# Stage 3 of a four-layer cross-attention kernel: rows normalised by quarters inside the last pair of heads, and MLP up and down projections interleaved

## What is computed

```python
def _cross_attention(q_in, kv_in, wq, bq, wk, bk, wv, bv, wo, bo, bias_k, bias_v):   # H=16 heads of K=128
    qh, kh, vh = (q_in @ wq + bq), (kv_in @ wk + bk), (kv_in @ wv + bv)               # split in heads
    kh, vh = concatenate([kh, bias_k]), concatenate([vh, bias_v])                     # one learned key and value
    weights = softmax(einsum('bqhk,bthk->bhqt', qh, kh) / sqrt(K))
    return einsum('bhqt,bthk->bqhk', weights, vh) @ wo + bo
x = x + _cross_attention(layer_norm(x, ln1), ctx, ...)       # sublayer 0
x = x + _cross_attention(layer_norm(x, ln2), ctx, ...)       # sublayer 1
h = layer_norm(x, ln_mlp)
x = x + gelu(h @ w_fc1 + b_fc1) @ w_fc2 + b_fc2              # 256 -> 1024 -> 256
```

## Time and profile before

| | us |
|---|---|
| median of 3 runs | 2165.06 (2163.31 to 2167.14) |
| the profiled execution | 2165.55 |
| its span, first to last instruction | 2163.9 |
| TensorE matmuls busy | 1952.3 (90%) |
| DVE busy | 1288.8 (60%) |
| ACT busy | 1189.3 (55%) |
| POOL busy | 678.0 (31%) |
| granted TensorE clock, mean | 0.966 of full |

### The profile page before, as it was taken

How to read it: one execution, slowest core, us unless ns; L and a number is a source line. 1 busy time by engine, 2 the same in 40 slices (tenths; PEclk the granted TensorE clock), 3 DMA queues, 4 the chain that set the end, 5 groups by cost and what they waited for, 6 DMA issues and landing times.

```text
span 2163.9 us, 43763 instructions
## 1 busy us (share of the span) xinstructions
PE 1952.3 (90%) x14880; PEld 1694.8 (78%) x14880; DVE 1288.8 (60%) x4117; ACT 1189.3 (55%) x3880; POOL 678.0 (31%) x618
## 2 busy tenths in 40 slices
PE   4678899999999988759999999997999999999788
PEld 3457677777777777548999999996899999999687
DVE  3578787878878764434555555556455555555654
ACT  2377787878778776535444444444444444444522
POOL 1233444444434343313222222132212122223444
PEclk8799999999999999869999999999999999999899
DMA  6000000000000000010000000000000000000100
GB/s 254 8 9 6 7 11 4 9 4 4 7 2 4 2 1 1 1 53 16 20 24 15 24 24 19 15 25 16 20 15 24 15 24 24 19 15 15 40 15 24
DMA packets 23663, 45.23 MB, mean 21 GB/s; under 512 B 2400, under 2 KB 10080, under 8 KB 22624
## 3 DMA queue, kind: packets, MB, share of 16 engines
q1 hardware_dynamic: 21440, 32.62, 5.0%
q10 hardware_dynamic: 1440, 8.72, 1.0%
q0 software_dynamic: 640, 2.10, 0.3%
HBM read 41.33 MB, written 2.10 MB: 20 GB/s over the span
## 4 chain that ended last, share of the span: by engine, by line
PE 44%; issue 5%; POOL 3%; DVE 2%; ACT 1%; DMA 0%; POOLq 0%; SPq 0%; DVEq 0%; ACTq 0%
PE general L1613 30%; PE o_psum L1662 5%; PE scores L1650 4%; PE pT_psum L1710 2%; PE general L1769 2%; POOL hT L1250 1%; DVE oT L1595 1%; POOL X L1275 1%; DVE oT L1464 1%; ACT oT L1374 0%; POOL w_qk L1235 0%; DMA raw_vrows<-vrows_dram 0%; POOL w_v L1235 0%; POOL probs L1259 0%; PE general L1624 0%
## 5 line engine op out<-in xcount | busy, mean ns | idle before, releaser
L489 POOL TENSOR_TENSOR probs<-probs,rsums 128x512 f32<-128x512 f32 (+1 forms) x288 | 282.7, 994 | 503.7 <-DVE rsums L691 502.9
L1259 POOL TENSOR_TENSOR probs<-probs,rsums 128x512 f32<-128x512 f32 x128 | 133.2, 1040 | 766.4 <-DVE rsums L1457 766.4
L525 ACT ACTIVATE probs<-negated,negmax 128x128 f32<-128x128 f32 (+1 forms) x768 | 325.4, 431 | 12.4 <-DVE negmax L682 12.1
L1366 ACT COPY probsT<-pT_psum 128x512 f32<-128x512 f32 x128 | 74.9, 585 | 291.1 <-PE pT_psum L1710 291.1
L964 PE MATMUL pT_psum<-ident,probs 128*128 128x128 f32 x1088 | 179.2, 287 | 58.4 <-ACT probsT L533 29.5
L964 PEld LDWEIGHTS pT_psum<-ident,probs 128*128 128x128 f32 x1088 | 127.2, 145 | 114.9 <-issue 68.4
L1613 PE MATMUL general<-hT,w_qk 128*128 128x512 f32 x768 | 207.3, 405 | 3.6 <-POOL hT L1250 3.6
L1613 PE MATMUL general<-w_o,oT 128*128 128x256 f32 x1536 | 195.0, 281 | 16.9 <-DVE oT L1464 16.9
L1613 PEld LDWEIGHTS general<-w_o,oT 128*128 128x128 f32 x1536 | 186.4, 188 | 25.1 <-DVE oT L1464 18.0
L1613 PE MATMUL general<-ctxT,w_qk 128*128 128x512 f32 x768 | 200.6, 397 | 0.0
L1358 ACT ACTIVATE probs<-scores,negmax 128x128 f32<-128x128 f32 x512 | 180.1, 369 | 29.9 <-DVE negmax L1449 29.7
(11 more groups left out here) (173 smaller groups left out, 3910.2 us busy)
## 6 DMA issues: line engine op xcount, KB each, us to landing
raw_qk<-w_qk_dram SPq DMA_DIRECT2D x34, 256.0 KB, 2.7
raw_v<-w_v_dram SPq DMA_DIRECT2D x17, 256.0 KB, 2.7
raw_vrows<-vrows_dram SPq DMA_DIRECT2D x17, 256.0 KB, 3.2
weights_a<-weights_a_dram ACTq DMA_DIRECT2D x2, 2048.0 KB, 18.1
raw_o<-w_o_dram SPq DMA_DIRECT2D x16, 256.0 KB, 2.6
weights_a<-weights_a_dram ACTq DMA_DIRECT2D x3, 1024.0 KB, 9.9
X<-x_dram SPq DMA_DIRECT2D x8, 256.0 KB, 7.8
ctx_in<-ctx_dram SPq DMA_DIRECT2D x8, 256.0 KB, 2.9
```

The costliest lines, as they stand in the source:

```text
L489: nc.gpsimd.tensor_tensor(pr, pr, rsums[:, n % 4, 0:segs].unsqueeze(2).broadcast_to([P, segs, width(kind) // segs]), ALU.mult).then_inc(s[ ...
L525: last = nc.scalar.activation(probs[:, n % PROBS, i * wide:(i + 1) * wide], src[:, i * wide:(i + 1) * wide], ACT.Exp, scale=1.0 if kind == ...
L1259: nc.gpsimd.tensor_tensor(pr, pr, rsums[:, t % 2, :].unsqueeze(2).broadcast_to([P, NB, P]), ALU.mult).then_inc(s["probs_ready"], 1)
```

## The change

1. The loop over sublayers is written out: `open` (first normalisation, as before), 7 pairs, the last pair of sublayer 0 (`turn`), 7 pairs, the last pair of sublayer 1 (`end`). In `turn` and `end` the normalisation of what follows goes by quarters. DVE makes the factors of quarter 0 in step 6 and of quarter 1 in step 7, ahead of that step's additions, those of quarters 2 and 3 around the last additions (`norm_rows`). TensorE transposes quarter 0 in step 7. Normalised rows and their transposed copy have buffers of their own (`xhat_turn`, `raw_hT_turn`), one quarter deep, since `qT` and `kT` are still in use.
2. `turn` keeps the usual table for steps 0 to 3, has keys `k` 3 and 4 in step 4 and `k` 5 behind two output groups in step 5; `q` 4 to 7, `k` 6 and 7 follow the pair, mixed with the last outputs, transposes and first scores.
3. In `end` the loads and splits of weights that nothing uses are left out. The up weights are split in steps 6 and 7 in halves, on ACT and POOL. The down weights are loaded into `kT` and split in halves on ACT and POOL; POOL's part stands after its five low parts of quarter 0.
4. The MLP's up groups of quarter 0 are mixed with the last outputs and the transposes. Then each up group of quarter g+1 is followed by the 12 down matmuls of quarter g for the same 128 hidden columns, into four banks that attention used (`down_sums`). Stores are issued by SP.

```diff
-    if last:
-        return [[*values[0], ("q", 0)], [*values[1], ("k", 0)], [*values[2], ("q", 1)], [*values[3], ("k", 1)],
-                [("q", 2), ("k", 2), ("q", 3)], [("k", 3), *outputs[0][:1]], [outputs[0][1], outputs[1][0]], [outputs[1][1], outputs[2][0]]]
+    if kind == "end":
+        return [[*values[0], ("q", 0)], [*values[1], ("k", 0)], [*values[2], ("k", 1)], [*values[3], ("q", 1)],
+                [("k", 2), ("k", 3), ("q", 2)], [("q", 3), *outputs[0]], outputs[1], [("ln", 0), outputs[2][0]]]
+    if kind == "turn":
+        return [[("q", 0), ("k", 0), *values[0]], [("q", 1), ("k", 1), *values[1]], [("q", 2), ("k", 2), *values[2]], [("q", 3), *values[3]],
+                [("k", 3), ("k", 4)], [*outputs[0], ("k", 5)], outputs[1], [("ln", 0), outputs[2][0]]]
...
+        xhat_turn = sb("xhat_turn3", [P, NB, D])
+        raw_hT_turn = sb("raw_hT_turn3", [P, KC, R])
...
+        down_sums = [scores[0], scores[1], pT_psum, o_psum]
...
# POOL
+                for g in range(G):
+                    for f in range(FC - LATE):
+                        up_low(g, f)
+                    if g == 0:
+                        for half in range(2):
+                            down_weights_low(half)
+                    add_biases(2, g)
...
# DVE
+                def norm_rows(a, g):
+                    norm_factors(slice(NB * g, NB * g + NB), None)
+                    if g > 0:
+                        wait_norm(dve, a, g - 1)
+                    dve.sem_inc(s["wait_passed"], 1)
+                    xhat_rows(a, g)
...
+                        if kind != "pair" and t >= G + 2:
+                            norm_rows(a + 1, t - G - 2)
+                        for key in pair_work(kind)[t]:
...
                     add_out(section, a, loop, G - 2, 1)
                     o_low(a, i, n, STEPS - 1)
-                    if not last:
+                    if kind == "pair":
                         front(n + 1, 0)
+                    else:
+                        norm_rows(a + 1, G - 2)
                     for j in range(2):
                         add_out(section, a, loop, G - 1, j)
+                    if kind != "pair":
+                        norm_rows(a + 1, G - 1)
...
# ACT, in the steps of pair
+                            elif key[0] == "ln":
+                                norm_copies(section, a + 1, 0, [1])
                         copy_pT(n)
+                        if kind != "pair" and t >= G + 2:
+                            xhat_rows(a + 1, t - G - 2)
...
# TensorE
+                pair(0, PAIRS - 1, "turn")
+                transposed("turn", 1, 1)
+                next_queries(4)
+                last_outputs("turn", 0, 0, ATT_UNITS - 1)
+                next_queries(5)
+                transposed("turn", 1, 2)
+                next_queries(6)
+                first_score("turn", 0, 0, ATT_UNITS - 1, [4])
+                keys("turn", 0, 0, 6, 0)
+                transposed("turn", 1, 3)
+                keys("turn", 0, 0, 7, 0)
+                next_queries(7)
...
+                pe.wait_ge(s["w_down_ready"], 2)
+                for g in range(G - 1):
+
+                    for f in range(FC):
+                        up(g + 1, (f,))
+                        wait_upT(g, f)
+                        for b in range(NB):
+                            last = down(g, f, b)
+                        last.then_inc(s["down_read"], 1)
```

More of the change, by code:

```diff
@@ L1299, in _ @@
-                pool.wait_ge(s["stored"], 2 * 16 * G)
+                            add_biases(a, t)
+                        if kind == "end" and t >= G + 2:
+                            up_weights_low(t - G - 2)
+                    if kind != "pair":
+                        for g in range(G):
+                            split_h(a + 1, g)
+                for g in range(G):
+                    split_h(0, g)
+                with pool.Fori(0, PAIRS - 1) as i:
+                    pair(0, i, "pair")
@@ L1348, in copy_q @@
+                    copy_q("open", 0, 0, G - 1, 0, 0)
                 def copy_q(section, a, i, t, head, pair):
@@ L1409, in _ @@
[L1409 to L1418 removed]
+                norm_open()
@@ new lines, in _ @@
+                copy_q("turn", 0, 0, 7, 0, PAIRS)
+                with act.Fori(0, PAIRS - 1) as i:
+                    pair(1, i, "pair")
+                pair(1, PAIRS - 1, "end")
+                norm_copies("end", 2, 1, [0, 1])
+                gelus(0, (0, 1))
+                xhat_rows(2, 2)
+                gelus(0, (2, 3))
+                norm_copies("end", 2, 2, [0, 1])
+                xhat_rows(2, 3)
+                gelus(0, (4, 5))
+                norm_copies("end", 2, 3, [1])
@@ L1420, in _ @@
+                gelus(0, (6, 7))
+                for half in range(2):
+                    down_weights_high(half)
+                for g in range(1, G):
+                    gelus(g, range(FC))
             @block.vector
@@ new lines, in next_queries, with up @@
+                def next_queries(t):
+                    pe.wait_ge(s["hT_ready"], t + 2)
+                    queries("turn", 0, 0, t, 0)
+                def up(g, fs):
+                    for f in fs:
+                        out, filled = wait_free(pe, "end", 1, 0, ("up", g, f))
+                        if f == 0:
+                            pe.wait_ge(s["hT_ready"], 2 * G + g + 2)
+                        split_matmul(out[:, :], lambda part, c: w_up[:, part, c, f * P:(f + 1) * P],
+                                     lambda part, c: hT[:, part, c, quarter(g)]).then_inc(filled, 1)
@@ L1774, in chunked @@
+                for b in range(NB):
+                    for f in range(FC):
+                        if b == 0:
+                            wait_upT(G - 1, f)
+                        last = down(G - 1, f, b)
+                    last.then_inc(s["down_read"], 1)
 def chunked(w):
```

502 lines of the change are left out of this document (283 added, 219 removed).

## The result

The changed kernel takes 2173.93 us, median of 8 runs (2170.33 to 2180.93), the one before 2164.6 us (2160.39 to 2167.14); the ratio is 1.0050, 95% interval 1.0037 to 1.0063. It is slower by 9.3 us. The forecast was 2175 us and slower, so the number came out. Not all of its reasons did: of the two profiled executions, 13.7 us apart (spans 2163.9 and 2177.6 us), stage 3, where the change is, is only 5.6 us longer in the later one.

What follows compares the result with a forecast made beforehand. The prediction saw stage 3's seams bound by a serial normalisation chain leaving TensorE some 46 us idle. Turn +7.5 and end with MLP +2.7 gave +10.2 us on 2165.06, forecast 2175 us, own range 2161 to 2182 (stated 2157 to 2184).

Steps and rivals of the forecast that it cites:

- Step 1: Turn, from the last pair's start to F6: new order of output and key groups costs +5.9 us, at least +5.0.
- F6: Reference point: the start of DVE's row maximum for softmax step 6 of the last pair; 1477.09 us before, in the turn.
- Steps 2 and 3: Turn, F6 to F7: factors ahead of additions on DVE +3.7 us; POOL holding DVE's small operations +1.8 (0 to 2).
- F7: Reference point: the start of DVE's row maximum for softmax step 7 of the last pair; 1483.47 us before, in the turn.
- Step 4: Turn, F7 to next pair: serial quarter chain and half clock take 39.0 us (36.5 to 41) against 42.9, -3.9.
- there is one buffer now and not two: Step 4's claim, in the turn: the next quarter's transposes stand behind the previous query because of one buffer; no separate size.
- Steps 5 to 7: Sublayer 1's end and MLP: F7 to 2029.8, then 47 us to first down matmul, then rest; +2.7 us (-6.6 to +6.5).
- Interleaving wins some 4 us and loses more ahead of them: MLP: mixing up and down groups wins some 4 us at the quarters and loses more ahead of them.
- Step 8: First pair loop: a table load, 7 times 1.28 us on ACT, is covered and costs nothing; uncovered up to 9 us.
- The chains are shorter: Rival, both last pairs and MLP: no POOL hold, no half clock, least hand-overs; -4.3 us, 2161 us; chance 0.20.
- TensorE's idle is filled: Last pairs: half the idle goes if F7 within 7 us of F6 and down weights ready; 2142 us, chance 0.13.
- POOL as the bound: MLP: casts and low parts exceed 7.11 us for five, delaying down matmuls up to 5 us; 2180 us; within slower's 0.67.

Runs made afterwards that it cites:

- e3: Changed kernel with POOL's splits (half of w_qk in turn, both halves of w_up in end) and their ACT casts moved to pair step 5: 2169.4 us, ratio 1.0018.
- e5: Changed kernel with the turn's transposes of quarter 3 right behind the third query, ahead of the first score and key group: 2170.8 us, ratio to before 1.0033.
- e7: Changed kernel with a second buffer for normalised and transposed rows of odd quarters in the end part, turn unchanged: 2176.6 us, ratio to before 1.0045.
- e9: Changed kernel with one Newton step instead of three in the factors of both seams' eight quarters: 2171.0 us, ratio to before 1.0020.
- e6: e2 with up and down projections not interleaved, all eight up groups of the next quarter first: 2163.8 us, ratio to before 0.9998.
- r_after: The changed kernel, unaltered, profiled and timed again in another group of runs: 2173.8 us, ratio to before 1.0044.
- e2: Changed kernel with the low-order down weights' casts (ACT) and subtractions (POOL) moved earlier, between the gelu low parts: 2165.6 us, ratio to before 0.9999.
- e4: Changed kernel with quarter 0's factors behind step 7's row maximum and sums on DVE, quarter 1's later too, in both last pairs: 2180.9 us, ratio 1.0063.
- c2: Changed kernel combining e1, e2 and the end's part of e3: 2151.5 us, ratio to before 0.9949.
- e1: Changed kernel with the seam between the sublayers put back as in the kernel before, end and MLP kept: 2165.6 us, ratio to before 0.9993.
- e8: Changed kernel with ACT's copy of the last unit's probabilities ahead of quarter 0's copy and cast, both last pairs: 2171.4 us, ratio to before 1.0022.
- c3: c2 plus the edit of e8, in the end alone: 2148.3 us, ratio to before 0.9908.

## Why the prediction was right, and where not

- *Step 1, up to F6.* Forecast +5.9, measured +4.3 (46.52 us from the start of the pair for 42.21). Steps 0 to 3 grew by 3.2 us, not by 4.1: three more groups cost less than three full ones, since the softmax matmuls between the groups of these steps took 2.4 to 2.7 us before the change and 2.2 after it. And the wait for DVE's low part shrank: step 5 takes 8.3 us, not 9.05.
- *Steps 2 and 3, F6 to F7.* Forecast 12, measured 11.55; in the end 12.9 forecast, 12.56 measured. The hold by POOL is 0.61 on `var` and 1.04 on `guess`, 1.65 for 1.8; e3 removed the second part by moving POOL's split (and the cast ahead of it on ACT) with DVE's instructions unchanged, so its cause is shown. The Trainium skill (SBUF — State Buffer, "SBUF: two separate sides") says that a DVE operation in a two-port mode or with two SBUF inputs and a GpSimd operation take the shared ports in turn, each for its whole instruction. The trace agrees: a held operation on 128x4 numbers ends with POOL's, within 0.03 us. `var`, `guess` and the normalised rows have one tensor as input and are held as well. Of the rule's two cases only the two-port mode can cover these, and no run shows in which mode an operation ran.
- *Step 4, F7 to the next pair.* Forecast 39.0, measured 40.9, so 2.0 won and not 3.9. Its hand-overs came as listed up to the third query (25.1 for 24.5). The mis-sized term is the half clock, +2.5 in all. It comes twice: query, score and key ahead of the transposes of quarter 3 run at half clock, so that these end at 32.3 and not at 29.4 (0.6 of it is the later third query); and the last query does so again behind its wait of 3.11 us (2.67 us, where e5's takes 1.65), so that from POOL's low part to the next pair it is 4.2 us for 2.2. And "there is one buffer now and not two" was wrong as a cause, as e7 shows for the end part; what keeps the quarters apart is DVE's factors (e9) and TensorE's order (e5).
- *The turn.* +7.5 forecast, +7.5 and +7.9 measured. Step 1 was 1.6 too high, steps 2 and 3 together 0.4, step 4 1.9 too low: that the sum fits to 0.1 us is luck, its sign and size are not.
- *Steps 5 to 7, the end.* F7 moved by 6.1 us (7.3 forecast), F7 to the first matmul after the wait is 48.7 (47), the rest 87.2 (80.1 + 2.2 + 3 + 4.5 = 89.8). So +0.6 us, not +2.7. The mis-sized terms are the query ahead of the outputs in step 5 (0.75 forecast; F6 comes 42.1 us after the pair's start in both), the five low parts (7.86 us for 7.11) and 0.5 us rounded off in step 6, and the tail, 3.0 us from the last matmul's end (2174.6) to the end of the span for 4.5. "Interleaving wins some 4 us and loses more ahead of them": the sum of the two is positive as forecast, though within the spread of a profile, and e6 shows that it is the quarter's lead that wins.
- *Step 8.* The table loads are there, 7 of 1.28 us, and the first seven pairs take 466.8 us for 467.6, and 466.8 to 469.5 in the other kernels: nothing beyond that spread, as forecast.
- *The sum.* +10.2 forecast for stage 3, +5.6 and +4.8 measured. In the first profile 2.1 of the missing 4.6 us are the end part, 0.8 the seven pairs of sublayer 0 and 1.7 those of sublayer 1 (445.9 us for 447.7; 444.8 in r_after), which the prediction left at nothing. As the same pairs take up to 447.5 us in the other kernels, this may be scatter. The time still met the forecast, since some 4 us came from ahead of stage 3. No step of the prediction has those; in so far the forecast was right by luck.
- *The rivals.* "The chains are shorter" did not happen: the hold by POOL came at nearly the forecast size, and the half clock cost more than forecast in the turn. "TensorE's idle is filled" did not happen, by its own condition: F7 came 11.55 us after F6, not within 7, and the down weights late. Its two conditions are not alike: with the second met (e2) the end part gained 11.7 us, with F7 at 7.08 us (e4) nothing was gained. "POOL as the bound" had 0.7 us of part in it (7.86 for 7.11); in e2 POOL does the same work and holds TensorE 1.6 us.

**What stays open.** The code ahead of stage 3 is the same in all these kernels, but stage 3 begins between 966.2 and 975.4 us. The differences arise in the first 220 us, where the granted clock differs too, and mostly persist from there on: POOL's 25th multiplication of probabilities starts at 128.3 us in before and 7.8 us later in after, its 288th at 912.2 and 7.9 later. The first 200 us of before and of after, in that order (two rows of each, columns as in the earlier trace rows):

```profile
0.00:100.00 100.00, 51.50 (x340) 36.98 (x340) 41.86 (x173) 30.52 (x108) 20.81 (x28) 0.86 0.38 141
100.00:200.00 100.00, 79.39 (x675) 63.47 (x676) 77.45 (x351) 67.41 (x259) 33.36 (x34) 0.92 0.03 9
```
```profile
0.00:100.00 100.00, 55.89 (x296) 39.29 (x296) 36.34 (x152) 29.93 (x106) 19.55 (x27) 0.78 0.38 141
100.00:200.00 100.00, 76.67 (x632) 61.35 (x632) 75.45 (x342) 60.40 (x226) 30.09 (x30) 0.91 0.03 8
```

The clock alone does not order them: c2, one of the earliest (966.5), has 0.82 in its first 100 us. Executions of one kernel scatter as much: those of e6 took 2158.9 to 2173.1 us, and the profiled one, whose stage 3 begins at 975.0, was the longest. Is the surplus tied to the new turn? In the four profiles with the old turn stage 3 begins at 966.2 to 968.4, in the ten with the new one at 966.7 to 975.4, median 971.5. A second reckoning (an estimate) takes for each kernel the difference of time by its ratio and subtracts the change of stage 3 in its profile. That leaves 5 us for after and r_after, but also 4.4 for c2 with the old turn, nothing for e1 with the old and for e6 and e8 with the new one, and -2.3 for c3; the others lie between 1.2 and 4.9. This ties the surplus to the turn at most loosely. What the 4 us of after and r_after are, no run tells.

## What to carry to other kernels

A reduction's finish that is split into quarters to start earlier adds a fixed chain for each quarter on the engine that finishes. Here four chains of factors in place of one put nearly three of them on the path, and the turn with them is 10 us longer than with the single wait that they replaced. When an engine is named as the releaser of a long wait, look at what stands ahead in its queue before calling it the bound: moving two subtractions (and their casts) won 11 us. When POOL's work is moved, see which small DVE instruction it will meet next. And when a change is worth a few us, compare the stretch that it touches, and look at an untouched one to see how much a single profile scatters.

## What the runs showed of the hardware

A DVE instruction on 128x4 numbers takes 0.17 us alone and 2.33 beside a POOL subtraction of 2.39 us: it is held until that ends. This was seen on `var`, `guess`, `negmax`, Newton steps, `shift` and normalised rows, all of which read and write on-chip memory outside the accumulator banks. One POOL instruction holds one of them, and those behind it run at their usual 0.17 us. Additions that read an accumulator bank, and the statistics, kept their 0.67 and 0.75 us (for two) at 1509.41 and 1510.12 of after, while POOL ran from 1509.27 to 1511.64. And the first 220 us of one and the same code differ by up to 8.8 us from one profiled execution to another.
